# Scan of an RWKV block on four 32x32 squares of the array, with a TensorE loop of two chunks, operands in two buffers, and early rows and values copied on ScalarE

## The chip, the cores and the metric

The kernel runs on one core of one Trainium2 chip. The metric is the device time of one launch in microseconds (us), of the slowest core, here the only one; of several runs the median is taken.

## The reference, cut to what matters

The program is one block of a network on a batch of 2 sequences, T = 4096 tokens, C = 256 channels, all in float32. An attention of the RWKV kind makes from each token six vectors per head (16 heads of 16 channels), runs a recurrence over the tokens, normalises and gates its output; two layers of local attention (windows of 128) with feed-forward parts follow. The change touches the recurrence alone:

```python
def step(s, inp):
    q_, w_, k_, v_, a_, b_ = inp
    sa = jnp.einsum('bhij,bhj->bhi', s, a_)
    s = s * w_[:, :, None, :] + sa[..., None] * b_[:, :, None, :] + v_[..., None] * k_[:, :, None, :]
    return (s, jnp.einsum('bhij,bhj->bhi', s, q_))
s0 = jnp.zeros((Bx, H, HS, HS), x.dtype)
_, y = jax.lax.scan(step, s0, (qt, wt, kt, vt, at, bt))
```

Each of the 32 heads (2 sequences of 16) has a state of 16x16, and each token's output depends on the state before it.

## The kernel before, in words

The program has six stages that follow one another: setup, mix (from tokens to the vectors q, w, k, v, a, b, which go to DRAM), **scan**, gate, local0 and local1. The change is in `scan_stage` (L857).

**Chunks.** The recurrence goes over 256 chunks of 16 tokens (`CH`). Within a chunk it is turned into products of small matrices. A unit has 4 chunks (`UC`), there are 64 units (`NU`), and a window w of 128 tokens has two, its halves k = 0 and 1. The 32 heads lie on 128 partitions (8 heads of 16 rows, `HP`) times 4 groups (`BG`, two sequences by two halves of the channels). To do several heads with one matmul, the operands are made block-diagonal: every head's 16 columns are multiplied with `headmask`, so that in a square of `QH` = 64 rows there stand `HQ` = 4 heads beside one another, each nonzero in its own rows only. One matmul call works in one square of the array, rows and columns 0 to 63 or 64 to 127 (`halves`), and a block of work of TensorE is 4 groups times 2 squares = 8 calls of 64x64 (`stacked`, L1134).

**A chunk on TensorE** (`chunk`, L1151) has ten blocks: P on the state (L1138, P<-state,ax), Y on the state (qx), Y on the values (d_qk), SA (p, d_t), S on the values (kT), the two blocks of `products` (L1120) for a chunk that is 16 chunks ahead (`LEAD` = 4 units), S on SA (bT), Y on SA (d_qb), and P on the values of the next chunk (`value_part`). The next state needs S; P needs the state; SA needs P; S needs SA. So the loop from state to state is P, SA, S and the copies and sums between them. TensorE's program holds one loop whose body is four chunks, and 16 chunks written out behind it, which have no products.

**The other engines.** ScalarE copies P, SA and Y from PSUM to SBUF (L1230, L1240, L1247), and makes the diagonals d_qk (`inner`) and d_qb (`outer`, both L1200) by four activations each, one for a head of the square; once per unit it takes squares and a root for the normalising of y. VectorE makes the diagonals d_ak and d_t (L1279), solves a triangular problem for a unit two ahead (a quarter of it per chunk, `solve`), adds S and the state (L1389), scales the sum to the new state, masks the products (`mask_products`), and normalises y once per unit. GpSimd makes ax and qx (L1071), bT and kT (L1092) for two chunks ahead (`use`) and bx and kx for 16 chunks ahead (`prepare`). SyncE issues all DMAs.

**What sets the order.** Every engine has its own program, written out by hand, and waits on semaphores. All but TensorE's are written by halves (`halfwise`): the body of their loop is a second half of one window and the first half of the next. SyncE's order in a unit is: load part, tt and gl of the next unit (L977, L1003, L968), load a problem (L992), in a second half store four heads of y (L1009); then for each pair j of chunks: load the early rows of five units ahead (`load_early`, L945, behind a wait for the products of the pair, ab_ps), load the values of the next unit (`load_v`, L952, behind a wait for the Y of the pair, y_ps), and with j = 0 the late rows; then the store of a solution (L997), the stores of the products (`pose`, L984 and L986), and in a first half four heads of y. The early rows lie in two buffers `early[j]`, the values in two buffers `v[j]`; both are read by TensorE where they lie. ax, qx, bT and kT have four buffers each, one for a chunk of the unit; bx, kx and the diagonals have two.

The waits ahead of the loads of early rows and of values are:

```python
sp.wait_ge(S["ab_ps"].sem, S["ab_ps"].after(first_chunk(w, k) + 2 * j + 1, UC))   # load_early
sp.wait_ge(S["y_ps"].sem, S["y_ps"].after(first_chunk(w, k) + 2 * j + 1, UC))     # load_v
```

`after(n, d)` is the count that a semaphore has once the step of chunk n - d is done.

## Time and profile before

| | |
|---|---|
| three runs | 5594.28, 5596.27, 5590.92 us |
| median | 5594.28 us |
| the profiled execution, its own time | 5591.23 us |
| its span, first to last instruction | 5589.4 us |
| mean granted TensorE clock | 0.960 |
| TensorE busy | 5148.8 us, 92% of the span |
| VectorE busy | 3842.0 us, 69% |
| ScalarE busy | 3335.5 us, 60% |
| GpSimd busy | 2734.8 us, 49% |

The busy times are means over six stages with different limits, so they tell little of the scan. The page has the span in 40 slices; in slices 9 to 16, the middle of the scan, it shows TensorE and GpSimd at 9 tenths or more. A row of a timeline stands for neighbouring instructions of one kind: x16 of `sc_P` is one block, since each float32 call of 64 columns is recorded as two passes. A row's duration is from the first start to the last end, so rows of a pipelined engine overlap, and the distance between starts is what a block costs. Releasers in brackets name what ended an idle time.

### The profile page before, as it was taken

What the parts mean: (1) busy time and instruction counts of PE and PEld (TensorE: products, weight loads), DVE (VectorE), ACT (ScalarE), POOL (GpSimd) and SP (SyncE); (2) the same over time, 40 slices, a digit from 0 to 9 for tenths busy, and PEclk for the clock granted to TensorE, in tenths of its full rate; (3) what the DMA queues carried; (4) which work ended last, traced back from release to release, by engine and by line L of the source; (5) the groups of instructions that cost most, each with busy time, mean ns of one, the idle gap of its engine ahead of it and who ended that gap; (6) DMA issues with size and microseconds to landing.
All of it is one profiled execution on the core that took longest, in us unless ns stands there. A gap on an engine that the chain in (4) does not pass through costs nothing. (4 is left out here: it accounts for less than half of the span.)

```text
span 5589.4 us, 195079 instructions
## 1 busy us (share of the span) xinstructions
PE 5148.8 (92%) x70040; PEld 4439.7 (79%) x70040; DVE 3842.0 (69%) x11245; ACT 3335.5 (60%) x9386; POOL 2734.8 (49%) x3844
## 2 busy tenths in 40 slices
PE   6888888799999999667999999999879999999999
PEld 5888887799999999545777777777757777777777
DVE  4666666698989999564666666666546666666665
ACT  4777777355555555444666666666546666666665
POOL 1222222799999999203444444444334444444443
PEclk8999998899999999888999999999989999999999
DMA  2333333666666766581000000000010000000000
GB/s 71 92 93 94 94 94 92 137 146 147 147 149 145 150 145 146 125 262 47 15 15 15 15 15 15 15 15 15 11 47 23 22 20 20 20 20 20 20 20 17
DMA packets 993634, 387.07 MB, mean 69 GB/s; under 512 B 773872, under 2 KB 938608, under 8 KB 992624
## 3 DMA queue, kind: packets, MB, share of 16 engines
q1 hardware_dynamic: 992304, 384.65, 28.8%
q14 instruction: 189, 1.55, 0.1%
q8 instruction: 53, 0.87, 0.1%
q10 hardware_dynamic: 1088, 0.00, 0.0%
HBM read 216.20 MB, written 168.30 MB: 69 GB/s over the span
## 5 line engine op out<-in xcount | busy, mean ns | idle before, releaser
L2166 ACT ACTIVATE l_prob<-l_prob,l_nb,l_rq 128x256 f32<-128x256 f32 x1024 | 604.9, 592 | 283.5 <-DVE l_nb L1967 281.3
L1830 POOL TENSOR_TENSOR l_pn<-l_prob,l_rinv 128x512 f32<-128x512 f32 x512 | 533.1, 1041 | 345.2 <-DVE l_rinv L1947 338.5
L1837 POOL TENSOR_TENSOR l_x1s<-l_x 128x128 f32<-128x128 f32 x128 | 58.2, 455 | 507.8 <-DVE l_x L1998 507.4
L1092 POOL TENSOR_TENSOR sc_kT<-sc_tok,sc_headmask 128x128 f32<-128x128 f32 x512 | 298.3, 601 | 0.0
L1200 ACT ACTIVATE sc_d_qk<-sc_part,sc_headmask 128x64 f32<-128x64 f32 x1024 | 270.4, 336 | 39.8 <-DMA sc_part<-scratch_part 39.8
L478 POOL TENSOR_TENSOR rk<-rk,bkraw 128x256 f32<-128x256 f32 x64 | 54.6, 873 | 478.0 <-DVE bkraw L364 478.0
L1092 POOL TENSOR_TENSOR sc_bT<-sc_tok,sc_headmask 128x128 f32<-128x128 f32 x512 | 278.2, 563 | 0.0
L1200 ACT ACTIVATE sc_d_qb<-sc_part,sc_headmask 128x64 f32<-128x64 f32 x1024 | 271.9, 339 | 0.0
L1854 POOL TENSOR_TENSOR l_outt<-l_t,l_xat 128x256 f32<-128x256 f32 x64 | 46.4, 725 | 453.2 <-DVE l_t L2030 453.2
L1842 POOL TENSOR_TENSOR l_dsqs<-l_dsq 128x128 f32<-128x128 f32 x128 | 58.5, 457 | 329.0 <-ACT l_dsq L2179 329.0
L473 POOL TENSOR_TENSOR xm<-tm,h 128x512 f32<-128x512 f32 x64 | 75.6, 1182 | 283.6 <-DVE tm L316 283.6
L1130 PE MATMUL sc_AB<-sc_early,sc_bx 64*64 64x64 f32 x4096 | 173.5, 221 | 42.0 <-POOL sc_kx L1071 34.4
L1071 POOL TENSOR_TENSOR sc_ax<-sc_late,sc_headmask 128x256 f32<-128x256 f32 x256 | 168.6, 659 | 76.7 <-PE sc_Y L1138 75.3
L1230 ACT COPY sc_p<-sc_P 128x64 f32<-128x64 f32 x256 | 54.5, 213 | 253.3 <-PE sc_P L1138 253.3
L1138 PE MATMUL sc_P<-sc_state,sc_ax 64*64 64x64 f32 x4096 | 173.8, 221 | 32.0 <-issue 30.1
L1247 ACT COPY sc_y<-sc_Y 128x64 f32<-128x64 f32 x256 | 54.5, 213 | 244.0 <-PE sc_Y L1138 244.0
L2166 ACT ACTIVATION_READ_ACCUMULATOR l_prob<-l_prob,l_nb,l_rq 128x1 f32 x1024 | 192.4, 188 | 0.0
L2362 PE MATMUL l0D<-l_hid,l_w 128*128 128x128 f32 x1536 | 192.4, 275 | 0.0
L2362 PE MATMUL l1D<-l_hid,l_w 128*128 128x128 f32 x1536 | 192.4, 275 | 0.0
L1130 PEld LDWEIGHTS sc_AB<-sc_early,sc_bx 64*64 64x64 f32 x4096 | 151.7, 138 | 43.4 <-issue 43.1
L1071 POOL TENSOR_TENSOR sc_qx<-sc_late,sc_headmask 128x256 f32<-128x256 f32 x256 | 182.9, 715 | 0.0
L1818 POOL TENSOR_TENSOR l_k<-l_kn,l_tab 128x512 f32<-128x512 f32 x128 | 162.8, 1272 | 40.6 <-DVE l_kn L1937 40.6
(364 smaller groups left out, 18138.5 us busy)
## 6 DMA issues: line engine op xcount, KB each, us to landing
scratch_cm<-cm SPq DMA_DIRECT2D x64, 512.0 KB, 4.1
sc_early<-scratch_cm SPq DMA_DIRECT2D x128, 256.0 KB, 3.3
scratch_part<-sc_att SPq DMA_DIRECT2D x64, 512.0 KB, 4.5
sc_part<-scratch_part SPq DMA_DIRECT2D x64, 512.0 KB, 4.3
scratch_tok<-vt SPq DMA_DIRECT2D x512, 48.0 KB, 1.8
l_h<-scratch_h SPq DMA_DIRECT2D x128, 129.0 KB, 2.6
scratch_gr<-gr SPq DMA_DIRECT2D x64, 256.0 KB, 2.0
sc_late<-scratch_cm SPq DMA_DIRECT2D x64, 256.0 KB, 3.7
```

The costliest lines, as they stand in the source:

```text
L473: nc.gpsimd.tensor_tensor(xm[b][:, 0:2], tm[b][:, 0:2], h[:, b, :, 1:P + 1].unsqueeze(1).broadcast_to([P, 2, CC, P]), ALU.add).then_inc(S[ ...
L1071: return nc.gpsimd.tensor_tensor(dst[:], src.unsqueeze(2).broadcast_to([P, BG, HQ, CH]), headmask[:].unsqueeze(1).unsqueeze(3).broadcast_t ...
L1092: last = nc.gpsimd.tensor_tensor(dst[c][:, b * CC:(b + 1) * CC], tok[k][:, c, b, x].unsqueeze(2).broadcast_to([P, CC, HQ, HS]), headmask[: ...
L1130: last = mm(bank[at, q * P + x * QH:q * P + (x + 1) * QH], src[c % 2][at, q].rearrange("p h t -> p (h t)"), rhs, start=True, stop=True)
L1138: ins = mm(bank[at, q * P:q * P + QH], lhs[at, q].rearrange("p h t -> p (h t)"), rhs[at, q].unsqueeze(1).broadcast_to([QH, HQ, HS]), start ...
L1200: last = nc.scalar.activation(dst[:, :, h, :], src, ACT.Copy, scale=headmask[:, h:h + 1])
L1818: tt(k1[s][:], kn[s][:], wide(2, slice(0, DH)), ALU.mult)
L1830: tt(pn[s][:, pair], prob[s][:, pair], rinv[s][:, pair].unsqueeze(2).broadcast_to([P, 2, 2 * P]), ALU.mult).then_inc(Q["pn"][s].sem, 1)
L1837: tt(x1s[s][:], shifted(x1[s][w])[:, 0:P], shifted(x1[s][w])[:, P:2 * P], ALU.add).then_inc(S["x1_sum"][s].sem, 1)
L1842: tt(dsqs[s][:], dsq[s][:, 0], dsq[s][:, 1], ALU.add).then_inc(S["dsq_sum"][s].sem, 1)
L2166: last_ = nc.scalar.activation(prob[s][:, h], prob[s][:, h], ACT.Exp, scale=rq8[s][:, h:h + 1], bias=nb[s][:, h:h + 1], accum_out=sums[s][ ...
L2362: last_ = mm(bank[s][3][:, c * P:(c + 1) * P], w2[:, m, c * P:(c + 1) * P], hid[s][:, m], start=(c == 0 and m == 0), stop=(c == CC - 1 and ...
```

## The change

The diff below has what matters of it. In words:

- `QH` becomes 32 (L34). A square is a quarter of the partitions, `HQ` is 2, the block-diagonal operands are 128 columns wide in place of 256, and a block is 4 groups times 4 squares = 16 calls of 32x32.
- ax, qx, bT and kT have two buffers in place of four; `use` waits for the Y of two chunks before. GpSimd does `prepare` ahead of `use` in each chunk.
- ScalarE makes two copies per chunk, `aq` (the early rows of the chunk whose products are next, 128 wide) and `vc` (the values of the next chunk, 64 wide), both with two buffers. TensorE reads these, `load_v` waits for the copy of the values in place of the Y.
- In PSUM the results of a block lie side by side, without gaps.
- TensorE's program has loops whose bodies are two chunks, three of them: the 16 products at the start, the 240 chunks with products, and 14 of the last 16; two chunks stand written out at the end.

```diff
-QH = 64
+QH = 32
...
-        ax, qx, bT, kT = ([sb(f"{n}{c}", [P, BG, HQ, CH]) for c in range(UC)] for n in ("ax", "qx", "bT", "kT"))
+        ax, qx, bT, kT = ([sb(f"{n}{c}", [P, BG, HQ, CH]) for c in range(2)] for n in ("ax", "qx", "bT", "kT"))
+        aq, vc = [sb(f"aq{k}", [P, BG, 2 * CH]) for k in range(2)], [sb(f"vc{k}", [P, BG, HS]) for k in range(2)]
...
                 def load_v(w, k, j):
-                    sp.wait_ge(S["y_ps"].sem, S["y_ps"].after(first_chunk(w, k) + 2 * j + 1, UC))
+                    sp.wait_ge(S["v_c"].sem, S["v_c"].after(first_chunk(w, k) + 2 * j + 1, UC))
...
-                    pool.wait_ge(S["y_ps"].sem, S["y_ps"].after(n, UC))
+                    pool.wait_ge(S["y_ps"].sem, S["y_ps"].after(n, 2))
...
                     for c in range(UC):
+                        if exists(w, k, LEAD):
+                            prepare(*shift(w, k, LEAD), c)
                         if c + 2 < UC:
                             use(w, k, c + 2)
                         elif exists(w, k, 1):
                             use(*shift(w, k, 1), c + 2 - UC)
-                        if exists(w, k, LEAD):
-                            prepare(*shift(w, k, LEAD), c)
...
-                halves = (slice(0, QH), slice(QH, P))
+                tiles = tuple(slice(at, at + QH) for at in range(0, P, QH))
...
                     pe.wait_ge(S["bk_x"].sem, S["bk_x"].after(m))
+                    pe.wait_ge(S["aq"].sem, S["aq"].after(m))
                     pe.wait_ge(S["att_sb"].sem, S["att_sb"].after(m, 2))
...
-                            for at in halves:
-                                rhs = early[c // 2][at, c % 2, 0, q // CC, q % CC].unsqueeze(1).broadcast_to([QH, 2, 2, CH])
-                                last = mm(bank[at, q * P + x * QH:q * P + (x + 1) * QH], src[c % 2][at, q].rearrange("p h t -> p (h t)"),
-                                          rhs, start=True, stop=True)
+                            for at in tiles:
+                                last = mm(AB_ps[c][at, (2 * q + x) * QH:(2 * q + x + 1) * QH], src[c][at, q].rearrange("p h t -> p (h t)"),
+                                          aq[c][at, q], start=True, stop=True)
...
-                        for at in halves:
-                            ins = mm(bank[at, q * P:q * P + QH], lhs[at, q].rearrange("p h t -> p (h t)"),
+                        for at in tiles:
+                            ins = mm(bank[at, q * QH:(q + 1) * QH], lhs[at, q].rearrange("p h t -> p (h t)"),
                                      rhs[at, q].unsqueeze(1).broadcast_to([QH, HQ, HS]), start=first and q == 0, stop=last_,
                                      skip_group_check=True)
...
-                    pe.wait_ge(pair["v_in"][c // 2].sem, pair["v_in"][c // 2].after(u))
+                    pe.wait_ge(S["v_c"].sem, S["v_c"].after(n))
...
-                with pe.Fori(0, NU - LEAD) as i:
-                    for c in range(UC):
-                        chunk(i, c, True, True)
-                for u in range(NU - LEAD, NU):
-                    for c in range(UC):
-                        chunk(u, c, False, u < NU - 1)
+                with pe.Fori(0, (NU - LEAD) * UC // 2) as i:
+                    for c in range(2):
+                        chunk(2 * i + c, c, True, True)
+                with pe.Fori((NU - LEAD) * UC // 2, NU * UC // 2 - 1) as i:
+                    for c in range(2):
+                        chunk(2 * i + c, c, False, True)
+                for c in range(2):
+                    chunk(NU * UC - 2 + c, c, False, c == 0)
...
+                def copy_aq(w, k, c):
+                    m = first_chunk(w, k) + c
+                    act.wait_ge(pair["early_in"][c // 2].sem, pair["early_in"][c // 2].after(w * 2 + k))
+                    act.wait_ge(S["ab_ps"].sem, S["ab_ps"].after(m, 2))
+                    nc.scalar.copy(aq[c % 2][:], bg(early[c // 2][:, c % 2, 0].rearrange("p b g y t -> p b g (y t)"))).then_inc(S["aq"].sem, 1)
+
+                def copy_v(w, k, c):
+                    n = first_chunk(w, k) + c
+                    act.wait_ge(pair["v_in"][c // 2].sem, pair["v_in"][c // 2].after(w * 2 + k))
+                    act.wait_ge(S["y_ps"].sem, S["y_ps"].after(n, 2))
+                    nc.scalar.copy(vc[c % 2][:], v[c // 2][:, c % 2]).then_inc(S["v_c"].sem, 1)
...
                     nc.scalar.copy(sa_sb[:], first16(SA_ps)).then_inc(S["sa_sb"].sem, 1)
                     if follow:
+                        copy_v(*nxt)
+                    if exists(w, k, LEAD):
+                        copy_aq(*shift(w, k, LEAD), c)
+                    if follow:
                         outer(*nxt)
```

**The order on ScalarE**, one chunk of the loop. Names are tiles: sc_p, sc_sa and sc_y are the copies of P, SA and Y, sc_part the solved parts from which the diagonals come. Before:

```order
L1230 COPY sc_p<-sc_P 128x64
L1200 ACTIVATE sc_d_qk<-sc_part,sc_headmask 128x4x16 x4
L1240 COPY sc_sa<-sc_SA 128x64
L1200 ACTIVATE sc_d_qb<-sc_part,sc_headmask 128x4x16 x4
L1247 COPY sc_y<-sc_Y 128x64
```

There the copy of SA is followed by the diagonals for the next chunk. In the changed kernel the same chunk reads:

```order
L1243 COPY sc_p<-sc_P 128x64
L1201 ACTIVATE sc_d_qk<-sc_part,sc_headmask 128x4x16 x2
L1253 COPY sc_sa<-sc_SA 128x64
L1226 COPY sc_vc<-sc_v 128x64
L1220 COPY sc_aq<-sc_early 128x128
L1201 ACTIVATE sc_d_qb<-sc_part,sc_headmask 128x4x16 x2
L1264 COPY sc_y<-sc_Y 128x64
```

The two new copies stand between the copy of SA and the second diagonals, the values first, and each diagonal has two pieces in place of four.

**The order on TensorE**, one chunk of the loop, from P on the state to P on the next values, without the register instructions between. Before:

```order
L1138 MATMUL sc_P<-sc_state,sc_ax 64x64 x8
L1138 MATMUL sc_Y<-sc_state,sc_qx 64x64 x8
L1138 MATMUL sc_Y<-sc_v,sc_d_qk 64x64 x8
L1138 MATMUL sc_SA<-sc_p,sc_d_t 64x64 x8
L1138 MATMUL sc_S<-sc_v,sc_kT 64x64 x8
...
L1130 MATMUL sc_AB<-sc_early,sc_bx 64x64 x8
L1130 MATMUL sc_AB<-sc_early,sc_kx 64x64 x8
L1138 MATMUL sc_S<-sc_sa,sc_bT 64x64 x8
L1138 MATMUL sc_Y<-sc_sa,sc_d_qb 64x64 x8
```

All ten blocks (the tenth is P on the next values) have 8 calls, and the products stand right before S on SA. In the changed kernel:

```order
L1138 MATMUL sc_P<-sc_state,sc_ax 32x32 x16
...
L1138 MATMUL sc_S<-sc_vc,sc_kT 32x32 x16
L1123 REGISTER_ALU
L1125 REGISTER_ALU
L1130 MATMUL sc_AB<-sc_aq,sc_bx 32x32 x16
L1130 MATMUL sc_AB<-sc_aq,sc_kx 32x32 x16
L1138 MATMUL sc_S<-sc_sa,sc_bT 32x32 x16
L1138 MATMUL sc_Y<-sc_sa,sc_d_qb 32x32 x16
```

The sequence of blocks is the same; each has 16 calls, and the products and the blocks on values read the copies `aq` and `vc`.

## Rows read from the trace of the kernel before

**Rows 1.** View by windows: the scan's steady stretch, its tail, 2.4 us within the tail.

```profile
1081.00:2225.00 1144.00, 1111.95 (x37191) 1100.85 (x37188) 1035.32 (x2382) 632.14 (x2735) 1088.63 (x1859) 1.00 0.68 147
2225.00:2307.00 82.00, 66.15 (x1947) 63.85 (x1942) 45.85 (x111) 39.70 (x172) 40.51 (x73) 0.94 0.33 64
...
2238.00:2240.40 2.40, 2.40 (x50) 2.40 (x48) 2.27 (x5) 0.48 (x3) 1.93 (x4) 0.50 0.03 7
```

**Rows 2.** Timeline of TensorE: start us, us, engine, line, operation, operands, count, [idle before <-releaser].

```profile
1433.85 0.66 PE L1138 MATMUL sc_S<-sc_sa,sc_bT 64*64 64x64 f32 x16
...
1434.99 0.68 PE L1138 MATMUL sc_P<-sc_v,sc_d_ak 64*64 64x64 f32 x16
1435.72 0.68 PE L1138 MATMUL sc_P<-sc_state,sc_ax 64*64 64x64 f32 x16
...
1437.14 0.66 PE L1138 MATMUL sc_SA<-sc_p,sc_d_t 64*64 64x64 f32 x16
```

**Rows 3.** The same view in the tail of the scan.

```profile
2236.32 0.50 PE L1138 MATMUL sc_S<-sc_v,sc_kT 64*64 64x64 f32 x10 [2.15 <-issue]
...
2237.13 0.31 PE L1138 MATMUL sc_Y<-sc_sa,sc_d_qb 64*64 64x64 f32 x1
2237.22 0.31 PE L1138 MATMUL sc_S<-sc_sa,sc_bT 64*64 64x64 f32 x1
...
2237.98 0.31 PE L1138 MATMUL sc_P<-sc_v,sc_d_ak 64*64 64x64 f32 x1
```

**Rows 4.** Timeline of VectorE, from the sum of one chunk to the second next.

```profile
1434.55 0.23 DVE L1389 TENSOR_TENSOR sc_ssum<-sc_S,sc_state 128x64 f32<-128x64 f32 x1 [0.64 <-PE sc_S L1138]
...
1435.71 0.83 DVE L1279 TENSOR_TENSOR sc_d_ak<-sc_part,sc_headmask 128x256 f32<-128x256 f32 x1
...
1439.71 0.23 DVE L1389 TENSOR_TENSOR sc_ssum<-sc_S,sc_state 128x64 f32<-128x64 f32 x1 [0.31 <-PE sc_S L1138]
...
1445.21 0.21 DVE L1389 TENSOR_TENSOR sc_ssum<-sc_S,sc_state 128x64 f32<-128x64 f32 x1
```

**Rows 5.** The same view, two chunks later.

```profile
1454.44 0.23 DVE L1389 TENSOR_TENSOR sc_ssum<-sc_S,sc_state 128x64 f32<-128x64 f32 x1
```

**Rows 6.** Timeline of SyncE's DMA issues, from one early load to the next.

```profile
1414.76 0.34 SPq L945 DMA_DIRECT2D sc_early<-scratch_cm  x1
1415.69 0.37 SPq L952 DMA_DIRECT2D sc_v<-scratch_tok  x1
...
1423.75 2.24 SPq L968 DMA_DIRECT2D sc_gl<-scratch_gl  x1
...
1426.88 2.94 SPq L1009 DMA_DIRECT2D scratch_y_tok<-sc_yn  x4
1430.19 0.34 SPq L945 DMA_DIRECT2D sc_early<-scratch_cm  x1
1430.87 0.39 SPq L952 DMA_DIRECT2D sc_v<-scratch_tok  x1
...
1434.28 0.34 SPq L945 DMA_DIRECT2D sc_early<-scratch_cm  x1
```

**Rows 7.** The same view, the early load that ends the window.

```profile
1454.17 0.35 SPq L945 DMA_DIRECT2D sc_early<-scratch_cm  x1
```

**Rows 8.** Timeline of TensorE in the first local stage: passes of 128 columns.

```profile
2708.05 1.95 PE L2354 MATMUL l0B<-l_hn,l_w 128*128 128x128 f32 x16
```

**Rows 9.** GpSimd's groups by line: the costliest of the steady scan; a local stage's of 128x128.

```profile
L1092 POOL TENSOR_TENSOR sc_kT<-sc_tok,sc_headmask 128x128 f32<-128x128 f32 x466 | 278.8, 617 | 0.0
...
L1837 POOL TENSOR_TENSOR l_x1s<-l_x 128x128 f32<-128x128 f32 x128 | 58.2, 455 | 507.8 <-DVE l_x L1998 507.4
```

**Rows 10.** Timeline of ScalarE in chunk D's predecessor.

```profile
1436.52 0.21 ACT L1230 COPY sc_p<-sc_P 128x64 f32<-128x64 f32 x1 [1.29 <-PE sc_P L1138]
...
1437.84 0.21 ACT L1240 COPY sc_sa<-sc_SA 128x64 f32<-128x64 f32 x1 [0.15 <-PE sc_SA L1138]
1437.95 1.06 ACT L1200 ACTIVATE sc_d_qb<-sc_part,sc_headmask 128x64 f32<-128x64 f32 x4
```

More of the change, by code:

```diff
@@ L1148, in value_part, with chunk @@
                     pe.sem_inc(s_pass, 1)
-                    stacked(P_ps, d_ak[c % 2], v[c // 2][:, c % 2], True, False)
-                def chunk(u, c, more, ahead):
-                    n = u * UC + c
-                    m = n + LEAD * UC
-                    s_in, values, Y = state[c % 2], v[c // 2][:, c % 2], Y_ps[c % 2]
+                    stacked(P_ps, d_ak[c], vc[c], True, False)
+                def chunk(n, c, more, follow):
+                    s_in, Y = state[c], Y_ps[c]
                     pe.wait_ge(S["ax_x"].sem, S["ax_x"].after(n))
@@ L1163, in chunk @@
                     pe.sem_inc(s_pass, 1)
-                    stacked(Y, d_qk[c % 2], values, False, False)
+                    stacked(Y, d_qk[c], vc[c], False, False)
                     pe.wait_ge(S["d_t"].sem, S["d_t"].after(n))
@@ L1179, in chunk @@
                     pe.sem_inc(s_pass, 1)
-                    stacked(Y, d_qb[c % 2], sa_sb, False, True).then_inc(S["y_ps"].sem, 1)
-                    if c < UC - 1 or ahead:
-                        value_part(n + 1, (c + 1) % UC, u + (c + 1) // UC)
-                for m in range(LEAD * UC):
-                    products(m, m % UC)
-                pe.wait_ge(s_state, 1)
-                value_part(0, 0, 0)
-                with pe.Fori(0, NU - LEAD) as i:
-                    for c in range(UC):
-                        chunk(i, c, True, True)
-                for u in range(NU - LEAD, NU):
-                    for c in range(UC):
-                        chunk(u, c, False, u < NU - 1)
+                    stacked(Y, d_qb[c], sa_sb, False, True).then_inc(S["y_ps"].sem, 1)
+                    if follow:
+                        value_part(n + 1, 1 - c)
+                with pe.Fori(0, LEAD * UC // 2) as i:
+                    for c in range(2):
+                        products(2 * i + c, c)
+                pe.wait_ge(s_state, 1)
+                value_part(0, 0)
+                with pe.Fori(0, (NU - LEAD) * UC // 2) as i:
[4 more added lines that the diff above has]
+                        chunk(2 * i + c, c, False, True)
+                for c in range(2):
+                    chunk(NU * UC - 2 + c, c, False, c == 0)
             @block.scalar
@@ L1250, in _ @@
                 act.wait_ge(s_c, 48)
+                for u in range(LEAD):
+                    for c in range(UC):
+                        copy_aq(u // 2, u % 2, c)
+                copy_v(0, 0, 0)
                 inner(0, 0, 0)
```

22 lines of the change are left out of this document (11 added, 11 removed).

## The prediction, made before the changed kernel had run

> **What bounds the kernel now.** I read the table by stage first. The change lies in the scan, and in its steady stretch (1081 to 2225 us, 1144 us) TensorE is busy 1112, GpSimd 1089 and VectorE 1035 us, ScalarE 632 [rows 1]. Three engines are near full, so a gain on TensorE alone would stop at the next one.
>
> The timeline of TensorE gives the unit of cost. A block (8 calls, 16 recorded passes) follows the one before by 0.47 us: from P at 1435.72 to SA at 1437.14 lie three, 1.42 us [rows 2]. A chunk has 10 of them, and P on the state opens the loop state to P to SA to S to state. Within a block the passes of the two squares overlap: where the trace shows an order, the first pass of Y (2237.13) starts before the last of S (2237.22), which stands ahead of it in the program [rows 3]. So each square has its own stream: 8 passes of 0.058 us make 0.47.
>
> The timeline of VectorE gives the four kinds of chunk, from one s_sum to where VectorE could do the next [rows 4]. I call them C (1434.55 to 1439.71, less the 0.31 that VectorE idles at its end: 4.85), D (1439.71 to 1445.21: 5.50, no wait ahead of the last row, so VectorE sets it), and A and B, together 9.23 (1445.21 to 1454.44) [rows 4, 5].
>
> The timeline of the DMA queue is what I read last, and it decides most. SyncE issues in program order. The long stretch lies in the second half of a window: after the early load at 1414.76 and its values at 1415.69 come the stores of the products, four heads of y, the two solved parts, gl (2.24 for itself), the problem, four more heads of y (2.94) and the next early load, and only then, at 1430.87, the values of the next window's first chunk [rows 6]. TensorE's P on those values starts at 1434.99, 1.14 after S at 1433.85 where two blocks would be 0.94, so they land just in time [rows 2]. From 1414.76 to that P are 20.23 us, once per window of 39.41 (1414.76 to 1454.17; second half 19.52 to 1434.28, first half 19.89 after it) [rows 6, 7]. In that half the queue is as slow as the engines.
>
> **The parts of the change.**
>
> *Squares of 32.* Calls per block double to 16, columns per pass halve. If all four squares overlap, a square still has 8 passes. Bounds from the rows: half a pass's time (0.029, block 0.23) and all of it (0.058, block 0.47). I take 0.25, near the half: 16 passes of 128 columns last 1.95, about 0.12 each, and 64 columns take 0.058 in their square, so time goes with columns [rows 2, 8].
>
> *Half the operand width.* The two diagonals of VectorE, 0.83 us each [rows 4], become 128 wide instead of 256: between nothing and half of 1.66 less. I take 0.85, the half, in C and 0.55 in D, where I read its other work as less slowed by GpSimd beside it. GpSimd does 4.7 us per chunk (1089 us; two kT groups a chunk, 466 in all, so 233 chunks) [rows 1, 9]. Its four groups of 256 become 128 wide, 0.46 by the local stage's row; the four of 128 become 64 wide, between half of 0.62 and all of it: 3.0 to 4.3. I take 3.3, under every chunk below [rows 9]. ScalarE loses 4 of 8 diagonal pieces (1.06 for four) and gains two copies [rows 10].
>
> *The two copies, and their place.* They stand between the copy of SA and the outer diagonals. The copy of the values has the width of the copy of SA, 0.21, and on its engine the next operation follows that one after 0.11 [rows 10]; the copy of the early rows is twice as wide, 0.27 by my estimate (0.21 to 0.42). So products can begin 0.54 after the copy of SA starts: 0.11, 0.11, 0.27 and a hand-over of 0.05. The products of chunk n now wait for a copy that ScalarE makes in chunk n, and S, which closes the state loop, is queued behind them. So the loop after sa is: copies 0.54, two product blocks 0.50, S. Before, TensorE's own queue covered it.
>
> *The loop of one chunk then.* s_sum and state, two of 0.23 [rows 4], with the restart of TensorE 0.59; P to its copy 0.80 now (1435.72 to 1436.52), less 0.23 for the shorter block 0.57; that copy and its hand-over 0.28; SA to its copy 0.70 now (1437.14 to 1437.84), 0.48; copies 0.54; products 0.50; S to s_sum 0.70 now (1433.85 to 1434.55), 0.48 [rows 2, 4, 10]. Together 3.44 us. VectorE in C is 4.85 - 0.85 = 4.0, in D 5.50 - 0.55 = 4.95. A has the root ahead of ScalarE's inner pieces, B has yn on VectorE: 3.8 and 3.9 as estimates between the loop's 3.44 and half of today's 9.23. One first half of a window: 4.0 + 4.95 + 3.8 + 3.9 = 16.65 us, against 19.89 now.
>
> *The value load.* The wait on y_ps becomes one on the copy, passed earlier: 0.25 us less (the issue of the values follows the end of the early one by 0.59 after 1414.76 and by 0.34 after 1430.19) [rows 6]. But the copy of the first values of a window is asked for in the chunk before, ahead of that chunk's products, which let SyncE issue the next early load. From early load to early load the second half therefore costs at least 20.23 - 0.25 = 19.98 to the values, both copies 0.38 (0.11 and 0.27), hand-over 0.05, products with their drain 0.69 (two blocks of 0.25 and what a last pass trails, estimated), SyncE 0.24: 21.3 us. The engines would need 15.7 (3.5 + 4.95 + 3.8 + 3.44). Now this half takes 19.5. **The change moves the late load from beside the loop into it, and that half gets longer.**
>
> Window: 21.3 + 16.65 = 38.0 against 39.4, -1.4.
>
> *The clock.* TensorE would idle some 5 us per window. In the tail an idle of 2.15 us is followed by a stretch at a granted clock of 0.50 (1.2 GHz of 2.4), with 0.85 from one block (2237.13) to the next (2237.98) instead of 0.47 [rows 1, 3]. The loop has five blocks on its path, each some 0.2 longer at half clock, so a chunk is 1 us longer; VectorE hides part in C. I charge 0.8 per window, between nothing and 1.6. Window 38.8, -0.6; times 29 windows: **-18 us**. (The Trainium skill, "TensorE: Matmul & The Clock Gate", Part 1, says that an idle stretch returns the array to half rate; the trace agrees with its 0.50 rows.)
>
> *The tail.* The last 16 chunks were unrolled and take 82 us: TensorE busy 66, so idle 16, VectorE busy 46 [rows 1]; one of the idle stretches is put down to nothing but issue [rows 3]. Now they loop and only two are unrolled. They have no products and no early copy, so the loop is 3.44 less 0.50 and 0.27, 2.7 a chunk or 43 in all, under VectorE's 46. I take VectorE's 46 and the 16 of waits as they are, 62: **-20 us**. If half of the waits go, -28; if the shorter blocks only lengthen the waits, 0. *Start of the scan:* shorter prepares, but loads and solving hide them: -2. *Loop branches:* 120 rounds instead of 60. The P at 1435.72 is the first block after one: 0.73 after the P on values instead of 0.47 [rows 2]. The branch stands in TensorE's program before the wait for the state, beside VectorE's two operations, so nothing; without that cover 0.26 for each of 60 more, 16 us.
>
> **Sum.** -18 - 20 - 2 = -40, from the profiled execution's 5591.2 (span 5589.4): **5551 us**. The median shown is 5594.3, 3 us above it.
>
> **The rivals.**
>
> *Four squares do not overlap* (slower). If passes start strictly in program order, a call's second pass holds up the next square: 0.029 and, as my estimate, 0.010 of hand-over per call, 16 calls 0.62 a block, 6.3 a chunk with the restart, 50.4 a window, +11 x 29 = +319, tail +5: 5915. It decides from a block of about 0.38 us, where the window is back at 39.4. Against it: the overtaking in [rows 3]; for it: only two squares are shown, never four. Chance 0.15. (The same page of the Trainium skill, Part 3, "What overlaps and what doesn't", says that matmuls start and end strictly in program order. By that rule the time would be this rival's; the rows above differ from it.)
>
> *Partial overlap or a pass that doesn't shrink fully*, block 0.30 to 0.467. At the upper end the loop is 4.9, the window 42.2, +81, tail -13: 5659; in the middle about 5620. Chance 0.17.
>
> *The values arrive in time* (the queue's issues, 2.24 for 8 KB of gl among them, shrink with less pressure). Then 15.7 + 16.65 = 32.4 a window, -7.0 x 29 = -204, with the tail 5365. Against it: it would need 4 us or more out of the 16.1 from 1414.76 to 1430.87, and the long rows of that stretch, 2.24 and 2.94, are the queue's own work and no waits [rows 6]. Chance 0.05.
>
> That the change doesn't do what it says is excluded by the order: 32x32, 16 calls.
>
> **How the numbers follow.** My case has 0.63, and its own bounds (clock, tail, diagonals) give 5515 to 5595. The range from 5490 to 5660 takes in the partial overlap and leaves out the first and third rival, 0.20. A difference of 0.2% (11 us) is about what a measurement of this kernel tells from none. Faster: 0.54 of mine, 0.05 of the third rival, 0.01 of the second: 0.60. Same: 0.08 and 0.02. Slower: 0.01 of mine, 0.14 and 0.15: 0.30.
>
> **What would show it.** Right: blocks start about 0.25 us apart, their passes interleaved; ScalarE's copy vc waits for sc_v once per window; SyncE's 16 us run unchanged; half clock behind that wait; first half near 16.7, second near 21.3; the tail near 60. Wrong: blocks over 0.38, a copy vc that never waits, or a chunk in which GpSimd or ScalarE is what TensorE waits for.

## The result, and the profile after

The changed kernel takes **5676.23 us** (median of 4 runs, 5675.65 to 5677.57), the kernel before 5593.71 in the same comparison: ratio 1.0148, interval 1.013 to 1.0166. It is slower by 1.5%, where the prediction had 0.7% faster. The profiled execution spans 5675.8 us against 5589.4, 86.4 us more.

By the starts of s_sum on VectorE, which open each chunk's end, these 86 us lie as follows. The 28 windows between chunk 16 and chunk 240 take 42.83 us each in place of 39.36: +97. The first two windows' worth before them is 9 longer, the last 16 chunks are 13 shorter (84.4 to 71.7), and what lies ahead of the scan and behind it is 7 shorter.

| | before | after |
|---|---|---|
| window of 8 chunks | 39.36 us | 42.83 us |
| mean granted TensorE clock | 0.960 | 0.925 |
| TensorE busy | 5148.8 us | 4933.0 us |
| VectorE busy | 3842.0 us | 3604.7 us |
| ScalarE busy | 3335.5 us | 3188.2 us |
| GpSimd busy | 2734.8 us | 2337.8 us |

Every engine has less to do and the time is longer, so the time went into waits. The view by windows (stretch, its length, then busy time and instructions of TensorE, its weight loads, VectorE, ScalarE and GpSimd, the granted clock, the DMA share, GB/s) shows the steady stretch, which answers to [rows 1], the last 16 chunks, and two short stretches at the two clocks:

```profile
1081.00:2295.00 1214.00, 906.77 (x72499) 854.04 (x72489) 802.82 (x2329) 488.40 (x2209) 711.30 (x1813) 0.85 0.64 135
2322.70:2395.40 72.70, 52.73 (x4213) 48.47 (x4209) 37.59 (x116) 29.58 (x135) 32.35 (x90) 0.83 0.37 72
...
1402.80:1404.60 1.80, 1.78 (x130) 1.80 (x134) 1.66 (x7) 0.69 (x3) 1.80 (x6) 0.50 0.86 195
1418.10:1419.10 1.00, 1.00 (x116) 0.96 (x104) 1.00 (x4) 0.47 (x3) 1.00 (x4) 1.00 0.90 160
```

No engine is near full any more: TensorE 75%, VectorE 66%, GpSimd 59% of 1214 us. The groups by line tell what TensorE waited for (behind the second bar):

```profile
L1130 PE MATMUL sc_AB<-sc_aq,sc_bx 32*32 32x32 f32 x8192 | 131.4, 205 | 321.6 <-ACT sc_aq L1220 160.3 <-POOL sc_kx L1072 152.7 <-DVE sc_att L1294 7.8
...
L1226 ACT COPY sc_vc<-sc_v 128x64 f32<-128x64 f32 x256 | 62.8, 246 | 48.6 <-DMA sc_v<-scratch_tok 48.6
```

Of the waits one stands out, 322 us ahead of the products, half of it put down to ScalarE's copy of the early rows and half to GpSimd's kx. The timeline of TensorE shows two such chunks, and blocks at full clock:

```profile
1411.15 0.42 PE L1130 MATMUL sc_AB<-sc_aq,sc_bx 32*32 32x32 f32 x29 [0.78 <-ACT sc_aq L1220]
1411.40 0.19 PE L1130 MATMUL sc_AB<-sc_aq,sc_kx 32*32 32x32 f32 x1
...
1416.31 0.42 PE L1130 MATMUL sc_AB<-sc_aq,sc_bx 32*32 32x32 f32 x29 [1.07 <-POOL sc_kx L1072]
...
1417.17 0.58 PE L1138 MATMUL sc_Y<-sc_sa,sc_d_qb 32*32 32x32 f32 x32
1417.81 0.45 PE L1138 MATMUL sc_P<-sc_vc,sc_d_ak 32*32 32x32 f32 x32
1418.11 0.45 PE L1138 MATMUL sc_P<-sc_state,sc_ax 32*32 32x32 f32 x32
1418.41 0.45 PE L1138 MATMUL sc_Y<-sc_state,sc_qx 32*32 32x32 f32 x32
1418.71 0.45 PE L1138 MATMUL sc_Y<-sc_vc,sc_d_qk 32*32 32x32 f32 x32
```

The four squares do overlap: 32 passes start in 0.30 us at full clock (1417.81 to 1418.71, three blocks). For the half put down to kx the cause is on GpSimd, whose timeline for the same chunks reads:

```profile
1412.61 0.40 POOL L1072 TENSOR_TENSOR sc_ax<-sc_late,sc_headmask 128x128 f32<-128x128 f32 x1 [1.97 <-PE sc_Y L1138]
...
1413.34 0.73 POOL L1093 TENSOR_TENSOR sc_bT<-sc_tok,sc_headmask 128x64 f32<-128x64 f32 x2
1414.03 1.33 POOL L1093 TENSOR_TENSOR sc_kT<-sc_tok,sc_headmask 128x64 f32<-128x64 f32 x2
1415.32 0.39 POOL L1072 TENSOR_TENSOR sc_bx<-sc_early,sc_headmask 128x128 f32<-128x128 f32 x1
1415.68 0.39 POOL L1072 TENSOR_TENSOR sc_kx<-sc_early,sc_headmask 128x128 f32<-128x128 f32 x1
1417.86 0.40 POOL L1072 TENSOR_TENSOR sc_ax<-sc_late,sc_headmask 128x128 f32<-128x128 f32 x1 [1.79 <-PE sc_Y L1138]
```

This is a closed ring. GpSimd waits for the Y of chunk n, because with two buffers that Y is the last reader of the ax, qx, bT and kT it writes for chunk n + 2 (`use`). Only then, in its own order, does it make bx and kx (`prepare`), which the products of chunk n + 1 need. S and Y of chunk n + 1 are queued behind these products, and its Y releases GpSimd again. Once round: 2.71 us for `use` (1412.61 to 1415.32), 0.75 for `prepare` (to 1416.07), 0.24 to the products (1416.31), 1.50 to the Y, which ScalarE copies at 1417.82 (below), and 0.05: **5.25 us a chunk**. GpSimd is idle for 1.79 of them, waiting for an engine that waits for it.

ScalarE's copies end almost as late:

```profile
1410.23 0.19 ACT L1253 COPY sc_sa<-sc_SA 128x64 f32<-128x64 f32 x1
...
1410.46 0.30 ACT L1220 COPY sc_aq<-sc_early 128x128 f32<-128x128 f32 x1
...
1415.02 0.21 ACT L1253 COPY sc_sa<-sc_SA 128x64 f32<-128x64 f32 x1
1415.13 0.25 ACT L1226 COPY sc_vc<-sc_v 128x64 f32<-128x64 f32 x1
1415.27 0.30 ACT L1220 COPY sc_aq<-sc_early 128x128 f32<-128x128 f32 x1
1417.82 0.21 ACT L1264 COPY sc_y<-sc_Y 128x64 f32<-128x64 f32 x1 [1.76 <-PE sc_Y L1138]
...
1421.46 0.24 ACT L1226 COPY sc_vc<-sc_v 128x64 f32<-128x64 f32 x1 [1.61 <-DMA sc_v<-scratch_tok]
```

aq is ready at 1415.57 and kx at 1416.07, half a us apart. Which of the two ends last changes from chunk to chunk: of 223 chunks of the steady stretch the products wait last for aq in 133 (152 us) and for kx in 90 (111 us). And once per window ScalarE waits for the values (1.61 us), with aq and so the products behind that. The DMA queue, which answers to [rows 6]:

```profile
1401.56 0.35 SPq L946 DMA_DIRECT2D sc_early<-scratch_cm  x1
...
1409.91 0.40 SPq L1004 DMA_DIRECT2D sc_tt<-scratch_inv  x1
1410.51 2.56 SPq L969 DMA_DIRECT2D sc_gl<-scratch_gl  x1
1413.41 0.33 SPq L993 DMA_DIRECT2D sc_prob<-scratch_att  x1
1413.96 2.95 SPq L1010 DMA_DIRECT2D scratch_y_tok<-sc_yn  x4
1417.27 0.34 SPq L946 DMA_DIRECT2D sc_early<-scratch_cm  x1
1417.95 0.39 SPq L953 DMA_DIRECT2D sc_v<-scratch_tok  x1
...
1423.64 0.34 SPq L946 DMA_DIRECT2D sc_early<-scratch_cm  x1
...
1444.14 0.35 SPq L946 DMA_DIRECT2D sc_early<-scratch_cm  x1
```

From the early load to the values are 16.39 us, 16.11 before. The second half of this window takes 22.08 us (1401.56 to 1423.64), the first half 20.50.

### The profile page after: what moved, and what is told of

Same layout as the page of the kernel before. It is cut to its first block and busy times, and to the rows that moved or that the text cites. A ratio compares the mean times of both kernels' runs of the same rounds, so it can differ in the third digit from the quotient of the medians.

```text
span 5675.8 us, 278008 instructions
## 1 busy us (share of the span) xinstructions
PE 4933.0 (87%) x111000; PEld 4178.0 (74%) x111000; DVE 3604.7 (64%) x11245; ACT 3188.2 (56%) x8874; POOL 2337.8 (41%) x3844
## 5 line engine op out<-in xcount | busy, mean ns | idle before, releaser
L1130 PE MATMUL sc_AB<-sc_aq,sc_bx 32*32 32x32 f32 x8192 | 131.4, 205 | 321.6 <-ACT sc_aq L1220 160.3
L1130 PEld LDWEIGHTS sc_AB<-sc_aq,sc_bx 32*32 32x32 f32 x8192 | 108.6, 118 | 343.9 <-issue 343.3
L1072 POOL TENSOR_TENSOR sc_ax<-sc_late,sc_headmask 128x128 f32<-128x128 f32 x256 | 104.5, 408 | 571.4 <-PE sc_Y L1138 571.4
L1410 DVE TENSOR_TENSOR sc_ssum<-sc_S,sc_state 128x64 f32<-128x64 f32 x256 | 57.4, 224 | 440.3 <-PE sc_S L1138 440.1
L1093 POOL TENSOR_TENSOR sc_kT<-sc_tok,sc_headmask 128x64 f32<-128x64 f32 x512 | 254.2, 515 | 0.0
L1863 POOL TENSOR_TENSOR l_dsqs<-l_dsq 128x128 f32<-128x128 f32 x128 | 58.8, 460 | 329.1 <-ACT l_dsq L2200 329.1
L2383 PEld LDWEIGHTS l0D<-l_hid,l_w 128*128 128x128 f32 x1536 | 181.5, 192 | 0.2 <-issue 0.2
L2383 PEld LDWEIGHTS l1D<-l_hid,l_w 128*128 128x128 f32 x1536 | 181.5, 192 | 0.2 <-issue 0.2
L1839 POOL TENSOR_TENSOR l_k<-l_kn,l_tab 128x512 f32<-128x512 f32 x128 | 162.6, 1271 | 40.9 <-DVE l_kn L1958 40.9
L1093 POOL TENSOR_TENSOR sc_bT<-sc_tok,sc_headmask 128x64 f32<-128x64 f32 x512 | 173.8, 358 | 0.0
L1138 PE MATMUL sc_P<-sc_state,sc_ax 32*32 32x32 f32 x8192 | 141.2, 211 | 37.2 <-POOL sc_qx L1072 19.8
```

Of the source, the lines that this page charges most:

```text
L1072: return nc.gpsimd.tensor_tensor(dst[:], src.unsqueeze(2).broadcast_to([P, BG, HQ, CH]), headmask[:].unsqueeze(1).unsqueeze(3).broadcast_t ...
L1093: last = nc.gpsimd.tensor_tensor(dst[c % 2][:, b * CC:(b + 1) * CC], tok[k][:, c, b, x].unsqueeze(2).broadcast_to([P, CC, HQ, HS]), headma ...
L1130: last = mm(AB_ps[c][at, (2 * q + x) * QH:(2 * q + x + 1) * QH], src[c][at, q].rearrange("p h t -> p (h t)"), aq[c][at, q], start=True, st ...
L1138: ins = mm(bank[at, q * QH:(q + 1) * QH], lhs[at, q].rearrange("p h t -> p (h t)"), rhs[at, q].unsqueeze(1).broadcast_to([QH, HQ, HS]), st ...
L1410: nc.vector.tensor_tensor(s_sum[:], first16(S_ps), state[c % 2][:], ALU.add).then_inc(S["s_sum"].sem, 1)
L1839: tt(k1[s][:], kn[s][:], wide(2, slice(0, DH)), ALU.mult)
```

## The experiments

**Theories.** G: GpSimd's ring sets the pace of most chunks. A: the place of the two copies on ScalarE does, as the prediction had it. V: the late values do. All kernels are edits of the changed one; each time is a median of 4 runs or more unless said. The kernel before, run again beside each group of them, had medians of 5591 to 5598 us, so a few us between two experiments say nothing.

### One chunk ahead on GpSimd, on ScalarE, on both

The first edit makes bx and kx one chunk earlier, ahead of `use` of the chunk before, still in two buffers (the diff shows the loop; the first bx and kx are made ahead of it):

```diff
                     for c in range(UC):
-                        if exists(w, k, LEAD):
-                            prepare(*shift(w, k, LEAD), c)
+                        if c + 1 < UC and exists(w, k, LEAD):
+                            prepare(*shift(w, k, LEAD), c + 1)
+                        if c + 1 == UC and exists(w, k, LEAD + 1):
+                            prepare(*shift(w, k, LEAD + 1), 0)
```

> Edit of the changed kernel: GpSimd makes bx and kx one chunk earlier, so before the ax to kT of the chunk before; two buffers stay. Theory G: as with four buffers, the wait for kx goes and the one for aq takes over, 5620 to 5640 us; the two runs are within 10 us of each other, since both cut the same chain. Theory A: 5670 to 5680.

Measured: 5627.23 us, 49 less than the changed kernel, window 40.9. The second edit does the same for the copy of the early rows, behind the second diagonals:

```diff
-                    if exists(w, k, LEAD):
-                        copy_aq(*shift(w, k, LEAD), c)
                     if follow:
                         outer(*nxt)
+                    if c + 1 < UC and exists(w, k, LEAD):
+                        copy_aq(*shift(w, k, LEAD), c + 1)
+                    if c + 1 == UC and exists(w, k, LEAD + 1):
+                        copy_aq(*shift(w, k, LEAD + 1), 0)
```

> Edit of the changed kernel: ScalarE copies the early rows one chunk ahead, behind the second diagonals, so no longer between SA and the products. Theory A: the products start after the copy of SA at once, window 42.8 to 40 or less, under 5600 us. Theory G: kx is ready as late as aq was, so almost nothing is won: 5650 to 5672 us, and the wait for kx grows to 250 us or more.

Measured: 5603.81 us, 72 less, window 40.2. That lies between what the two theories gave: neither G nor A holds alone. The groups by line of the two kernels, the one with GpSimd ahead first:

```profile
L1133 PE MATMUL sc_AB<-sc_aq,sc_bx 32*32 32x32 f32 x8192 | 127.2, 202 | 299.1 <-ACT sc_aq L1223 164.7 <-POOL sc_kx L1072 124.9 <-DVE sc_att L1297 8.7
```

```profile
L1130 PE MATMUL sc_AB<-sc_aq,sc_bx 32*32 32x32 f32 x8192 | 128.6, 203 | 255.5 <-POOL sc_kx L1072 244.3 <-DVE sc_att L1297 8.0 <-ACT sc_aq L1220 1.3
```

With aq ahead its wait is gone (160 to 1.3 us) and the one for kx grows from 153 to 244, as G had it. With kx ahead its wait only falls to 125, for a reason that the one edit makes itself: bx one chunk earlier is closer behind the load of the early rows, and GpSimd waited 46 us for these in the steady stretch.

The distance from one start of the products to the next shows what each branch costs by itself. With aq ahead, kx comes last in about 190 of the 223 chunks, and chunks that wait for it follow one another by 5.16 us (median): GpSimd's ring. With kx ahead, aq comes last in 187, and these follow one another by 4.75 us: a second bound right behind the first. kx is then waited for about once per window, in the chunk with the late values, which takes 7.34 us here and 5.19 with aq ahead. The edit with both:

> Both edits together. Theory G with A behind it: neither kx nor aq is waited for, most chunks fall to 4 to 4.9 us, and what remains is the load of the values once per window, window about 38.5, 5540 to 5580 us. If each had been a bound of its own, the two gains would add; if they are two branches that end within half a us of each other, the sum of the two single gains is less than half of this one's. Theory of the clock (half clock makes the time, whatever the waits): over 5640.

Measured: **5500.15 us**, 176 less than the changed kernel and 97 less than the one before as it ran beside it (ratio 0.9827, 0.981 to 0.9843). The gain is larger than the theory had (5540 to 5580). The single gains, 49 and 72, make 121, 69% of 176. So the two branches hide each other in part, but less than I expected (under half). The wait ahead of the products falls from 322 to 74 us:

```profile
L1133 PE MATMUL sc_AB<-sc_aq,sc_bx 32*32 32x32 f32 x8192 | 125.8, 200 | 73.8 <-POOL sc_kx L1072 34.7 <-issue 27.7 <-DVE sc_att L1300 7.7
...
L1229 ACT COPY sc_vc<-sc_v 128x64 f32<-128x64 f32 x256 | 62.9, 246 | 134.3 <-DMA sc_v<-scratch_tok 134.2
```

and the wait for the values grows from 49 to 134 us. The chunks of a window take 3.65 to 4.51 us each but for the one with that load, 8.46. The theory that the clock makes the time whatever the waits (over 5640) falls.

### Does GpSimd's ring scale as it should?

The changed kernel with squares of 64 again, and VectorE reading the products in PSUM as before for it (the diff shows TensorE's side), all else as changed:

```diff
-QH = 32
+QH = 64
...
-                                          aq[c][at, q], start=True, stop=True)
+                                          aq[c][at, q].unsqueeze(1).broadcast_to([QH, 2, 2 * CH]), start=True, stop=True)
```

> The changed kernel with squares of 64 (operands 256 wide again), all else as changed: order, copies, two buffers. Theory G: GpSimd's use takes 3.7 us and prepare 1.4 by the durations before the change, and from the products to the Y lie four blocks of 0.47 and the drain, so each chunk takes about 7.3 us: window near 58, 6050 to 6200 us. Rival (GpSimd's order does not bind, TensorE does): 10 blocks of 0.47 and little more, window 40 to 44, 5600 to 5720.

Measured: 6151.74 us (2 runs), window 58.8, so 7.35 a chunk: the ring with the old durations. The products wait for kx in all 223 chunks of the steady stretch. TensorE's blocks are again 8 calls of 64x64, as before the change, and the kernel is 10% slower than before it. Its trace, GpSimd and then TensorE:

```profile
1507.13 0.61 POOL L1072 TENSOR_TENSOR sc_ax<-sc_late,sc_headmask 128x256 f32<-128x256 f32 x1 [3.73 <-PE sc_Y L1138]
...
1511.00 0.61 POOL L1072 TENSOR_TENSOR sc_kx<-sc_early,sc_headmask 128x256 f32<-128x256 f32 x1
```

```profile
1511.85 0.35 PE L1130 MATMUL sc_AB<-sc_aq,sc_bx 64*64 64x64 f32 x5 [1.85 <-POOL sc_kx L1072]
```

### Four buffers, and a loop of four chunks

The straight way to break the ring is to give ax, qx, bT and kT their four buffers back. TensorE's loop has to be four chunks long for that (its edit is the one of the next experiment).

```diff
-        ax, qx, bT, kT = ([sb(f"{n}{c}", [P, BG, HQ, CH]) for c in range(2)] for n in ("ax", "qx", "bT", "kT"))
+        ax, qx, bT, kT = ([sb(f"{n}{c}", [P, BG, HQ, CH]) for c in range(UC)] for n in ("ax", "qx", "bT", "kT"))
...
-                    pool.wait_ge(S["y_ps"].sem, S["y_ps"].after(n, 2))
+                    pool.wait_ge(S["y_ps"].sem, S["y_ps"].after(n, UC))
```

> Edit of the changed kernel: ax, qx, bT and kT have four buffers again and use() waits for the Y of four chunks before; TensorE's loop body is four chunks for that. Theory G (GpSimd's new chain: Y of a chunk, then ax, qx, bT, kT into the buffer it frees, then bx and kx, then the products of the next chunk, then its Y): the wait of the products for kx (153 us in all) goes, the wait for aq (160 us) stays and takes a part over, window 42.8 to about 41, 5620 to 5640 us. Theory A (the place of the early copy on ScalarE is all that matters): no change, 5670 to 5680. Theory V (the load of the values alone): no change.

Measured: 7263.11 us. No theory had that, so the loop was tried alone, with two buffers:

```diff
-                with pe.Fori(0, (NU - LEAD) * UC // 2) as i:
-                    for c in range(2):
-                        chunk(2 * i + c, c, True, True)
+                with pe.Fori(0, NU - LEAD) as i:
+                    for c in range(UC):
+                        chunk(UC * i + c, c, True, True)
```

> The changed kernel with a TensorE loop of four chunks in place of two, two buffers as changed. With four buffers and this loop the time was 7263 us, with idle stretches of 2 to 3 us that wait for nothing shown, in any block, and 783 packets in the instruction queue against 42. Theory L (the body, 640 calls in place of 320, is too long to stay in the engine and is fetched again in every round): the same 7250 to 7300 us. Rival (the four buffers did it): 5670 to 5690.

Measured: 7248.28 us (one run). The loop does it, not the buffers: one run, but within 15 us of the 7263, where the rival had 5690. The view by windows and the timeline of TensorE:

```profile
1300.00:3800.00 2500.00, 1156.94 (x68694) 1055.60 (x68686) 767.31 (x2206) 463.94 (x2090) 666.72 (x1715) 0.50 0.31 66
```

```profile
1703.76 0.44 PE L1138 MATMUL sc_Y<-sc_vc,sc_d_qk 32*32 32x32 f32 x15
1706.17 0.44 PE L1138 MATMUL sc_Y<-sc_vc,sc_d_qk 32*32 32x32 f32 x17 [1.97 <-issue]
...
1711.11 0.48 PE L1130 MATMUL sc_AB<-sc_aq,sc_kx 32*32 32x32 f32 x19 [2.44 <-issue]
...
1715.17 0.49 PE L1138 MATMUL sc_P<-sc_state,sc_ax 32*32 32x32 f32 x20 [2.00 <-issue]
```

TensorE stops in the middle of a block, for about 2 us, waiting for nothing that the profile shows. Its queue of instructions, in this kernel and then in the changed one (packets, MB, share of the DMA engines):

```profile
q8 instruction: 783, 12.83, 0.8%
```

```profile
q8 instruction: 42, 0.69, 0.1%
```

The 741 packets more are about 12 for each of the 60 rounds, 16.4 KB each, and the stalls lie a fixed length of program apart: from the one at 1706.17 to the one at 1711.11 are 125 passes, and again to 1715.17, with as many weight loads beside them. So the body is fetched anew in every round. In the changed kernel a round has 320 calls, as many as before the change (4 chunks of 80), and it stays in the engine. At 640 it does not, and a window costs 93 us: 48 us of idle put down to issue (1350 us in the 28 windows), and the rest at a granted clock of 0.50. (The Trainium skill, "Runtime: NRT & Kernel Launch", section "Instruction fetch mechanics", says that TensorE holds 2048 instructions, refilled in blocks of 16 KiB, and that a taken branch to a page that is not held forces a fetch. The packets of 16.4 KB agree. At two weight loads and two passes per call the bodies have, by estimate, 1280 and 2560 instructions, on either side of its figure. It also calls the cost of crossing such a block mostly hidden; here it is about 2 us each time.) So the loop of two chunks belongs to squares of 32, and with it the buffers must be chosen by c % 2. The ring can be broken by order, not by four buffers.

### The values first

SyncE issues the four stores of y of a second half behind the late rows, no longer ahead of the early rows:

```diff
-                    if k and len(heads):
-                        store_y(w - 1, heads)
                     for j in range(UC // 2):
...
+                        if j == 0 and k and len(heads):
+                            store_y(w - 1, heads)
```

> Edit of the changed kernel: SyncE issues the four stores of y of a second half after the values of the next window and the late rows, not before the early rows; nothing else. Theory V (the late values cost 1.6 us once per window, behind GpSimd's chain): the wait of ScalarE's copy of the values goes, window 42.8 to about 41.3, 5625 to 5650 us. Theory G alone: the wait is beside the chain over GpSimd, no gain, 5665 to 5680.

Measured: 5629.26 us, 47 less, window 41.1. So the late values, 1.6 us once per window, lie on the path also where the ring sets the pace: the chunk with them falls from 6.18 to 5.14, the one behind it from 5.38 to 4.76. With both copies ahead as well:

> Both copies ahead (bx, kx and the early rows one chunk earlier) and the values first. With both ahead the last chunk of a window took 8.46 us, where the others take 3.7 to 4.5, and ScalarE waited 4.5 us for the values there. Theory V: the values come 3.3 us earlier, and so does the chunk: window 36.9 to about 33.8, 5390 to 5420 us. Rival (VectorE or GpSimd is right behind): less than half of that, 5450 to 5490.

Measured: 5435.4 us, window 34.7. The theory had 80 to 110 us less than with both copies ahead, and 65 came, which lies between it and its rival. Part of the rest is in a wait that the edit makes itself: the stores go out later, and VectorE writes `yn` for the next window only when they have landed:

```profile
1528.40 0.42 DVE L1403 TENSOR_TENSOR sc_yn<-sc_dev,sc_rs 128x256 f32<-128x256 f32 x1 [2.60 <-DMA scratch_y_tok<-sc_yn]
```

VectorE then normalises a first half one chunk later, at the start of the next window, before `dev` is overwritten:

```diff
                         if c == 0:
+                            if not k:
+                                normalised(*shift(w, k, -2))
                             deviations(*before)
...
-                        if c == 2 + k:
+                        if c == 2 and not k:
                             normalised(*before)
```

> All three edits with squares of 32, and VectorE normalises the first half of a window one chunk later, at the start of the next window. With all three, VectorE waited 2.6 us there for the stores of y to land, which the edit of SyncE's order had made later, and the last chunk of a window took 6.06 us against 4.13 in the other half. Theory: that wait goes, window 34.7 to about 33, 5375 to 5400 us. Rival (the load of the values, 1.15 us there, takes its place): 5405 to 5430.

Measured: **5412.82 us** (5408.5 to 5415.4; ratio to before 0.968, 0.9664 to 0.9696), window 33.9. That is the rival's value: the 2.6 us are gone, and a wait for the values, 1.15 us until then, is 2.07.

### What the squares of 32 are worth

The edit of `QH` as above, with both copies ahead and the values first.

> All three edits with squares of 64, so TensorE with ten blocks of 0.47 per chunk and operands 256 wide. It tells what the squares of 32 are worth once the new waits are gone (5435 us with squares of 32). Theory: TensorE's 4.67 per chunk and VectorE's 5.5 in one of four set the pace again, window 39.5 to 41, 5590 to 5650 us, so the squares are worth 150 to 210 us. Rival (the squares are worth little, the order of issue made the gain): under 5500.

Measured: 5566.93 us (ratio 0.9956, 0.994 to 0.9973), window 39.3, with TensorE busy 1049 of 1080 us at full clock. Against 5435 with squares of 32 and the same three edits, the squares, with the narrower operands that come with them, are worth 132 us once the waits are gone; the theory had 150 to 210, and 5590 to 5650 us for this kernel. The three edits on squares of 64 win 0.4% over the kernel before. That is not won in the windows, which are as long as before (39.3 and 39.4): 16 of the 26 us lie in the tail, whose last 15 chunks take 64.0 us in TensorE's new loops, 80.2 before.

### The values before gl

Last, the load of the first pair's values was moved up to right behind tt, and that of the second pair ahead of its early rows:

```diff
                         load_t(*n1)
+                        load_v(*n1, 0)
                         load_gl(*n1)
...
+                        if j == 1 and exists(w, k, 1):
+                            load_v(*shift(w, k, 1), j)
                         if exists(w, k, LEAD + 1):
                             load_early(*shift(w, k, LEAD + 1), j)
-                        if exists(w, k, 1):
-                            load_v(*shift(w, k, 1), j)
```

> The fastest so far (5413 us) with one more change of SyncE's order: the values of the next unit's first pair are loaded right behind tt, ahead of gl, the problem and the early rows, since the copies have freed their buffer a chunk earlier; those of the second pair ahead of their early rows. There ScalarE waited 2.07 us for values in a second half and 0.4 to 0.9 in the other. Theory V: the waits go, window 33.9 to about 32, 5350 to 5375 us. Rival (with the values there, the early rows or VectorE end as late): under 15 us of gain, 5398 to 5415.

Measured: 5412.3 us, no gain: the rival. SyncE's queue with the values at their old place, and in this kernel:

```profile
1509.79 0.41 SPq L1004 DMA_DIRECT2D sc_tt<-scratch_inv  x1
1510.39 2.44 SPq L969 DMA_DIRECT2D sc_gl<-scratch_gl  x1
...
1514.55 0.38 SPq L953 DMA_DIRECT2D sc_v<-scratch_tok  x1
```

```profile
1510.15 2.62 SPq L953 DMA_DIRECT2D sc_v<-scratch_tok  x1
1512.96 0.37 SPq L969 DMA_DIRECT2D sc_gl<-scratch_gl  x1
...
1514.39 0.33 SPq L946 DMA_DIRECT2D sc_early<-scratch_cm  x1
```

The long issue did not move with gl. It stayed behind tt, in every unit of the steady stretch: gl there took 2.13 to 3.77 us before the change (47 units), the values there 2.08 to 3.81 (54 units), and gl behind the values 0.36 or 0.37. The wait of ScalarE for the values is gone (52.3 us in all to 0.1), and the early rows, issued as late as ever, are waited for in its place:

```profile
L1224 ACT COPY sc_aq<-sc_early 128x128 f32<-128x128 f32 x256 | 73.3, 288 | 87.2 <-DMA sc_early<-scratch_cm 73.8 <-PE sc_AB L1134 13.1
```

That the next issue pays for tt because the queue is still full of tt's small pieces is my reading; it was not tested by a different tt.

## Why the prediction was wrong

**The failed step.** The prediction counted GpSimd as a load: "I take 3.3, under every chunk below". The sum of its work was about right (711 us busy in 227 chunks of the steady stretch, 3.1 each). What it had wrong is the wait. It left out that `use` now waits for the Y of two chunks before instead of four, and that the products wait for what GpSimd does behind `use`. The change that I listed as a narrower operand is also a new ring. The same rows would have given it: `use` two groups of 0.46 and four between 0.31 and 0.62, 2.2 to 3.4; `prepare` 0.9; four blocks of my 0.25 and a trail of 0.2: 4.3 to 5.5 a chunk, where my loop had 3.44. Measured: 5.25, and 5.16 where nothing but the ring is left. The prediction's own sign of being wrong, a chunk in which TensorE waits for GpSimd or ScalarE, is what the trace shows.

**A second step, mis-sized.** The loop over ScalarE's copies was 3.44 us in the sum. With the ring opened it shows by itself, at 4.75. In the chunks of that run that wait for aq, the products start 0.92 us after the copy of SA (forecast 0.54), P on the state 0.71 after s_sum (0.59), and SA 0.52 after the copy of P (0.28), with TensorE's two blocks of Y and VectorE's d_t between them (medians of 187 chunks; which of the two holds SA back was not tested). So without the ring, too, the first half would have been longer than forecast: 18.8 us on average in that run, for 16.65.

With `prepare` and the copy both one chunk ahead, chunks take 3.65 to 4.5 us, a first half 16.0 and a second 20.9, close to the 16.65 and 21.3 forecast. That agreement is partly luck: those figures had the copy of the early rows inside the loop, and 4.95 for VectorE's longest chunk, where now the longest but the one with the load is 4.51 (medians over the windows).

**Point by point.**

- *Squares of 32 overlap.* Right, and the rival that they do not falls: the first pass of kx starts among the last of bx (the x1 at 1411.40 above), as [rows 3] had it for two squares. The size was off: a block takes 0.30 at full clock, not 0.25 (bounds 0.23 and 0.47), and 0.42 at half clock. That is the lower edge of the second rival. Time does not go with columns down to 32.
- *Half the operand width.* Right: VectorE's diagonals are 128 wide, and the profile puts 0.9 us of waiting in all to them.
- *The two copies.* The place was read rightly as the new bound of some chunks: 160 us of waiting, 72 us of time when it is moved. Where aq is last, the products start 0.92 us after the copy of SA does (1410.23 to 1411.15), for 0.54 forecast: aq ends on time at 0.53, and the hand-over, with the first weights, takes 0.39, for 0.05 in the sum. Moving it wins more than opening the ring does (72 us against 49), but the one hides the other: both together win 176.
- *The value load.* Right: ScalarE's copy waits for it once per window (1.61 us), the queue's stretch is unchanged (16.4 us), the second half is 22.1 us long where 21.3 was forecast, and the edit of the queue alone wins 47 us. The first half is the failure, 20.5 for 16.65.
- *The clock.* Under-sized. It falls to 0.85 in the steady stretch, from 1.00 [rows 1], where TensorE idles a quarter of it and not an eighth, and it is back at 0.97 in the fastest version, where TensorE is 88% busy. It does not follow the idle share alone: with the values first it is 0.93, at the same 75% busy. Its own share of the 3.5 us per window was not measured apart.
- *The tail.* -12.7 us for a forecast of -20 (0 to -28). The idle by issue of [rows 3] is not gone from it, 15.1 us in the last 15 chunks, 14.7 before; it now lies in the first round of the loop without products and in the two chunks written out (`2390.74 0.32 PE L1138 MATMUL sc_Y<-sc_state,sc_qx 32*32 32x32 f32 x4 [2.69 <-issue]`). With squares of 64 in the same loops and all three edits this idle is 2.1 us and the 15 chunks take 64.0, with squares of 32 and the same edits 67.5. So the squares of 32 do not shorten the tail but lengthen it. That it is shorter than before for the loops in place of written-out code fits the idle, but was not tested apart. The clock in it is 0.83, where it was 0.94.
- *Loop branches* cost nothing that a run shows: with squares of 64 and all three edits TensorE makes 120 rounds and the window is 39.3, for 39.4 with 60.
- *Slower* had a chance of 0.30, for other reasons: the time of the second rival, 5659 at its upper end, was near, by a mechanism (a block near 0.47) that the trace excludes. That the measured time is close to it is chance.

So TensorE had its gain, 132 us. What ate it and more: GpSimd's ring and the copies, 176 us together, and the late values behind them, 65 more once these are gone. The remaining 26 are what the same edits win with squares of 64: 5594 - 26 - 132 + 65 + 176 = 5677.

## What to carry to other kernels

When a buffer count falls, draw the ring that the new wait closes, through every engine's own order, and add up once round; an engine that is busy for 60% of the time can set all of it. What is made for 16 chunks ahead is cheap to make one chunk earlier still, and here the places of one copy and one `prepare` decided over more (176 us) than halving TensorE's columns won (132). When two rings have nearly the same length, an edit that opens one of them wins little, and only both together show what they cost. Before a loop body is lengthened or its calls doubled, count the instructions of one round and look at the packets of the instruction queue.

## What the runs showed that I had not expected

- **A loop body that TensorE does not hold.** 640 calls per round in place of 320: 741 more packets of 16.4 KB, a window of 93 us in place of 43, 28% more time in all, with 1350 us of stalls in the steady stretch put down to nothing but issue, and half clock from end to end of it.
- **A DMA's issue is paid by its neighbour.** The 2.24 us that I read in [rows 6] as gl's own are what stands behind tt: with the values there, these take 2.62 and gl 0.37, and so in every unit. A long row in the DMA queue is to be asked first what was issued before it.
- **A pass of 32 columns does not take half of one of 64.** 32 passes on four squares take 0.30 us at full clock, 16 on two squares 0.47: halving the columns gave 0.64 of the time.
